# Row sums added to acc by GpSimd instead of VectorE, with every stored row at twice its value until ScalarE halves it in the last pass

## The reference, cut to what matters

```python
def _L0_rec_ref(x, beta, W, b):      # x 2048x512, beta 1024x8x512, W 1024x512, b 1024
    s = einsum('bn,hln->bhl', x, beta)
    ssq = einsum('bn,hln->bhl', x * x, beta * beta)
    fm = 0.5 * sum(s * s - ssq, axis=-1)
    return fm + x @ W.T + b
```

## Time and profile before

| | |
|---|---|
| median of 3 runs | 789.49 us (788.95 to 790.73) |
| the profiled execution, its own time | 789.54 us |
| its span in the trace | 787.8 us |
| busy: PE / PEld / DVE / ACT / POOL | 98% / 80% / 71% / 52% / 47% |
| DMA moved | 145.35 MB, 185 GB/s in the mean |

### The profile page before, as it was taken

The page is one execution under the profiler, slowest core; times in us unless marked ns, Lnnn a source line. Parts: engine busy times, 40 slices in busy tenths (PEclk is TensorE's granted clock), DMA queues, the critical chain, the costliest instruction groups (busy, mean ns, idle before and its releaser), DMA issues. The chain is left out here.

```text
span 787.8 us, 9817 instructions
## 1 busy us (share of the span) xinstructions
PE 774.3 (98%) x3382; PEld 633.7 (80%) x3382; DVE 559.4 (71%) x646; ACT 410.2 (52%) x564; POOL 369.1 (47%) x328
## 2 busy tenths in 40 slices
PE   8999999899999999999999999999999999989998
PEld 5887878688888888888888888888888888867886
DVE  6899468976666666666666765766576656699995
ACT  5665355455554555455555555555555545553330
POOL 0133175446554654465346545653556355434443
PEclk9999999999999999999999999999999999999999
DMA  9596963085624561466046515651663166438933
GB/s 342 212 383 251 363 213 104 15 326 161 228 87 146 199 223 34 147 214 214 27 154 220 208 32 172 229 177 31 218 229 125 47 220 214 148 95 312 382 128 152
DMA packets 66738, 145.35 MB, mean 185 GB/s; under 512 B 4864, under 2 KB 41728, under 8 KB 64384
## 3 DMA queue, kind: packets, MB, share of 16 engines
q1 hardware_dynamic: 66688, 144.72, 52.0%
HBM read 102.76 MB, written 41.94 MB: 184 GB/s over the span
## 5 line engine op out<-in xcount | busy, mean ns | idle before, releaser
L443 PE MATMUL bank<-t_hi,s_hi 128*128 128x512 f32 x1116 | 436.6, 391 | 8.1 <-ACT r L593 3.7
L447 PE MATMUL bank<-t_lo,s_hi 128*128 128x512 f32 x1124 | 438.1, 390 | 0.4 <-DVE t_lo L691 0.2
L449 PE MATMUL bank<-t_hi,s_lo 128*128 128x512 f32 x1116 | 434.7, 390 | 0.0
L443 PEld LDWEIGHTS bank<-t_hi,s_hi 128*128 128x128 f32 x1116 | 209.8, 188 | 57.8 <-ACT r L593 4.5
L447 PEld LDWEIGHTS bank<-t_lo,s_hi 128*128 128x128 f32 x1124 | 211.4, 188 | 44.3 <-DVE t_lo L691 1.0
L449 PEld LDWEIGHTS bank<-t_hi,s_lo 128*128 128x128 f32 x1116 | 209.8, 188 | 43.8
L954 POOL TENSOR_TENSOR r<-r 128x512 f32<-128x512 f32 x70 | 109.7, 1567 | 261.9 <-ACT r L605 261.9
L817 DVE TENSOR_REDUCE sums<-cs 128x128 f32<-128x1024 f32 x128 | 155.4, 1215 | 69.6 <-ACT cs L624 68.7
L801 DVE TENSOR_TENSOR cs<-bank,r 128x512 f32<-128x512 f32 x70 | 48.4, 691 | 85.4 <-PE bank L449 84.9
L958 POOL TENSOR_TENSOR cs<-r 128x512 f32<-128x512 f32 x70 | 92.7, 1324 | 22.0 <-issue 17.0
L950 POOL TENSOR_TENSOR acc<-acc,bias_all 128x128 f32<-128x128 f32 x128 | 60.8, 496 | 87.2 <-DMA acc<-acc_kept 87.1
(11 more groups left out here) (53 smaller groups left out, 343.6 us busy)
## 6 DMA issues: line engine op xcount, KB each, us to landing
s_hi<-s_hi_kept SPq DMA_DIRECT2D x30, 896.0 KB, 5.2
s_lo<-s_lo_kept SPq DMA_DIRECT2D x30, 896.0 KB, 6.9
t_lo_in<-beta_p SPq DMA_DIRECT2D x16, 1024.0 KB, 7.1
s_lo_in<-x_p SPq DMA_DIRECT2D x16, 512.0 KB, 4.3
acc_kept<-cs SPq DMA_DIRECT2D x16, 512.0 KB, 5.4
acc<-acc_kept SPq DMA_DIRECT2D x64, 128.0 KB, 4.8
acc_kept<-acc SPq DMA_DIRECT2D x64, 128.0 KB, 1.8
s_hi_kept<-s_hi SPq DMA_DIRECT2D x8, 896.0 KB, 6.1
```

The costliest lines, as they stand in the source:

```text
L443: nc.tensor.matmul(to, s_hi[:, slot, s_op, cols], hi[:, k, :], start=start, stop=False, skip_group_check=True)
L447: nc.tensor.matmul(to, s_hi[:, slot, s_op, cols], lo[:, k, :], start=False, stop=False, skip_group_check=True)
L449: return nc.tensor.matmul(to, s_lo[:, slot, s_op, cols], hi[:, k, :], start=False, stop=stop, skip_group_check=True)
```

## The change

- All rows that are kept in DRAM hold twice their value. In the W pass ScalarE multiplies by 2 instead of copying, and VectorE's three additions of a bank become one `scalar_tensor_tensor` each (bank times 2 plus the other operand). ScalarE doubles the bias once.
- In the main passes line 823 of VectorE is gone. GpSimd adds `sums` to `acc` in one instruction over 128x256, in group g+1, behind the bias for g+1 and ahead of r5 + r7 of g+1. For group 71 it stands in group 72, behind line 969.
- In the Q pass ScalarE halves each `f` in place, one instruction over 128x2048. The first stands behind `square_row2(71)`, the others at the end of a group for the next one. GpSimd's and VectorE's first use of an `f` waits for that.
- SyncE issues the first six loads of `f` ahead of `store_acc(71)`, where it was two.

```diff
@@ SyncE, Q pass
                 if i == 0:
-                    load_f(0)
-                    load_f(1)
+                    for other in range(6):
+                        load_f(other)
                     store_acc(FIRST_Q - 1)
-                    for other in range(2, 6):
-                        load_f(other)
@@ ScalarE
-                nc.scalar.copy(cs[:, g, row, half, :], bank(g, place)).then_inc(direct_copied, 1)
+                nc.scalar.mul(cs[:, g, row, half, :], bank(g, place), 2.0).then_inc(direct_copied, 1)
+
+            def copy_of(g, to, place):        # used by copy_r1, copy_r5, copy_r7; C11 in the same way
+
+                if g < FIRST_MAIN:
+                    return nc.scalar.mul(to[:, :], bank(g, place), 2.0)
+                return nc.scalar.copy(to[:, :], bank(g, place))
+
+            def halve_f(i):
+                act.wait_ge(f_loaded[i], 16)
+                nc.scalar.mul(f_at(i), f_at(i), 0.5).then_inc(f_halved, 1)
...
                 if g >= FIRST_MAIN:
                     square_12(g)
+                elif g == FIRST_MAIN - 1:
+                    act.wait_ge(bias_loaded, 16)
+                    nc.scalar.mul(bias_all[:, :], bias_all[:, :], 2.0).then_inc(bias_doubled, 1)
             for g in range(FIRST_Q, GROUPS):
                 copy_r1(g)
                 if g == FIRST_Q:
                     square_row2(g - 1)
+                    halve_f(0)
                 for other in groups_for(SUMMED_IN, g):
                     square_x(other)
                     split_s(other)
+                if g + 1 < GROUPS:
+                    halve_f(g + 1 - FIRST_Q)
@@ VectorE
+            def add_from(g, to, place, other):     # used by add_r2, add_c12, add_c21
+
+                if g < FIRST_MAIN:
+                    return nc.vector.scalar_tensor_tensor(to, bank(g, place), 2.0, other[:, :], ALU.mult, ALU.add)
+                return nc.vector.tensor_tensor(to, bank(g, place), other[:, :], ALU.add)
...
@@ VectorE, sum_rows
-                dve.wait_ge(row2_summed, m + 1)
-                dve.wait_ge(acc_biased, m + 1)
-                nc.vector.scalar_tensor_tensor(acc[:, g % 2, :, :], sums[:, :, :], 0.5, acc[:, g % 2, :, :],
-                                               ALU.mult, ALU.add).then_inc(acc_added, 1)
@@ VectorE, Q pass, line 901
-                dve.wait_ge(f_loaded[i], 16)
+                dve.wait_ge(f_halved, i + 1)
@@ GpSimd
+            def add_sums(g):
+
+                m = g - FIRST_MAIN
+                pool.wait_ge(acc_biased, m + 1)
+                pool.wait_ge(row1_summed, m + 1)
+                pool.wait_ge(row2_summed, m + 1)
+                nc.gpsimd.tensor_tensor(acc[:, g % 2, :, :], acc[:, g % 2, :, :], sums[:, :, :], ALU.add
+                                        ).then_inc(acc_added, 1)
...
                     made.then_inc(acc_biased, 1)
+                    if m:
+                        add_sums(g - 1)
                 pool.wait_ge(r5_copied, count(g))
...
-                pool.wait_ge(f_loaded[i], 16)
+                pool.wait_ge(f_halved, i + 1)
...
                 nc.gpsimd.tensor_tensor(f[:, 1, COLS:], f[:, 1, COLS:], r5[:, :], ALU.add).then_inc(o22_added, 1)
+                if i == 0:
+                    add_sums(g - 1)
```

More of the change, by code:

```diff
@@ L213, in fm_layer @@
         row2_summed = sem("row2_summed")
+        bias_doubled = sem("bias_doubled")
+        f_halved = sem("f_halved")
         acc_biased = sem("acc_biased")
@@ L592, in copy_r1 @@
                     act.wait_ge(r2_added, count(g - 1))
-                nc.scalar.copy(r1[:, :], bank(g, BANK_A)).then_inc(r1_copied, 1)
+                copy_of(g, r1, BANK_A).then_inc(r1_copied, 1)
             def copy_r5(g):
@@ L598, in copy_r5 @@
                     act.wait_ge(c22_added, count(g - 1))
-                nc.scalar.copy(r5[:, :], bank(g, BANK_E)).then_inc(r5_copied, 1)
+                copy_of(g, r5, BANK_E).then_inc(r5_copied, 1)
             def copy_r7(g):
@@ L604, in copy_r7 @@
                     act.wait_ge(r57_added, count(g - 1))
-                nc.scalar.copy(r7[:, :], bank(g, BANK_D)).then_inc(r7_copied, 1)
+                copy_of(g, r7, BANK_D).then_inc(r7_copied, 1)
             def take_c11(g):
@@ L610, in take_c11 @@
                 if g < FIRST_MAIN:
-                    nc.scalar.copy(cs[:, g % 2, 0, 0, :], bank(g, BANK_A)).then_inc(c11_taken, 1)
+                    nc.scalar.mul(cs[:, g % 2, 0, 0, :], bank(g, BANK_A), 2.0).then_inc(c11_taken, 1)
                 else:
@@ L794, in add_r2 @@
                     dve.wait_ge(c22_added, count(g - 1))
-                nc.vector.tensor_tensor(r2[:, :], bank(g, BANK_B), r1[:, :], ALU.add).then_inc(r2_added, 1)
+                add_from(g, r2[:, :], BANK_B, r1).then_inc(r2_added, 1)
             def add_c12(g):
@@ L800, in add_c12 @@
                 wait_cs_free(dve, g, 0)
-                nc.vector.tensor_tensor(cs[:, g % 2, 0, 1, :], bank(g, BANK_E), r2[:, :], ALU.add
-                                        ).then_inc(c12_added, 1)
+                add_from(g, cs[:, g % 2, 0, 1, :], BANK_E, r2).then_inc(c12_added, 1)
             def add_c21(g):
@@ L806, in add_c21 @@
                 wait_cs_free(dve, g, 1)
-                nc.vector.tensor_tensor(cs[:, g % 2, 1, 0, :], bank(g, BANK_D), r2[:, :], ALU.add
-                                        ).then_inc(c21_added, 1)
+                add_from(g, cs[:, g % 2, 1, 0, :], BANK_D, r2).then_inc(c21_added, 1)
             def sum_rows(g):
@@ L945, in _ @@
                     if m == 0:
-                        pool.wait_ge(bias_loaded, 16)
+                        pool.wait_ge(bias_doubled, 1)
                     pool.wait_ge(acc_loaded[g % 2], 16 * (m // 2 + 1))
```

## The result

The changed kernel took 806.42 us (median of 4 runs, 804.49 to 807.04) against 789.30 for the kernel before; the ratio is 1.0204, with a 95% interval of 1.0185 to 1.0222. That is 17.1 us more; the forecast was 803, 13.35 more, in a range of 793 to 809. The profiled execution took 804.49 us with a span of 802.7, 14.9 longer than before. The other executions of this kernel were up to 2.6 us longer.

The account below looks back on a forecast made before the run. TensorE was taken to bound the kernel. W pass 0.1, groups 9 to 13 5.0, groups 66 to 72 4.0 and Q pass 4.25 summed to 13.35 us on 789.54, so 803 us; range 793 to 809.

Parts of the forecast that it names:

- What bounds: Whole kernel: TensorE, busy 98% of the span; time saved or spent elsewhere counts only where TensorE waits.
- the three places of the earlier trace: TensorE's losses near groups that prepare an x: 2.31 us at 144.31, 1.35 at 700.31, 1.19 at 723.43.
- the wait at 144.31: TensorE's 2.31 us behind ScalarE's copy of r1, said to cost more as the clock then fell to 0.57.
- The loop: Main passes: addition waits for bias and acc load; nothing in six passes, 5.0 us in groups 9 to 13.
- Price of the addition: GpSimd's new addition over 128x256, taken as 0.75 us, between 0.50 and 1.32.
- Groups 66 to 72: Late stores of acc delay the x for 72 and 73: 4.0 us, bounds 1.5 and 6.
- The meeting with line 691: Groups 66 to 72: GpSimd's addition meets VectorE's line 691 right behind the row sums, 1.2 us.
- The halving: Q pass: ScalarE halves f, 1.91 us each; cycle near 9.98 us, five more groups lose 0.41 each, 2.05.
- The mis-sized term: Start of the Q pass: first f halved before use, making `add_r2(73)` late by 2.2 us, within 1.4 to 2.7.
- Only the Q pass: Rival: load and bias don't bind and x comes in time; 794, or 796 with half another term; chance 0.18.
- Contention everywhere: Rival: collisions with line 691 reach steady passes, or new waits drop the clock; 8 to 10 us more, 812; chance 0.09.
- Faster: Rival: VectorE's relief shrinks the 144.31 wait by 1.9 us, clock holds, Q pass cost hidden; 785.5; chance 0.06.

Follow-up runs that it names:

- e12: Kernel before, all work where it was, but SyncE's store of acc for g-1 also waits for the bias for g: 794.74 us, ratio 1.0058.
- e3: Changed kernel, but GpSimd adds the sums for g-1 ahead of the bias for g, not behind it: 797.65 us, ratio 1.0100.
- e1: Changed kernel, but VectorE keeps the addition of the sums; doubling, halving and new order of f loads stay: 795.40 us, ratio 1.0065.
- e2: Kernel before with the addition on GpSimd behind the bias, one half put into ScalarE's squares, no doubling or halving: 800.80 us, ratio 1.0137.
- e7: e2 with GpSimd's addition ahead of the bias: 793.49 us, ratio 1.0045.
- e11: e7, but VectorE adds for groups 69 to 71 and GpSimd for the other 61: 791.68 us, ratio 1.0024.
- e5: Changed kernel, but ScalarE halves the next group's f ahead of its split of x, not behind it: 804.33 us, ratio 1.0171.

## Why the prediction was right, step by step

- **What bounds.** Right: TensorE, near the three places of the earlier trace rows and nowhere else. 456.96 us of steady passes are equal to the hundredth. Not right is that the wait at 144.31 "costs more than its length" by the fall of the clock; see the last section.
- **The loop.** Right, with its cause shown: e12 has the wait and no work (4.9 us), e3 the work and no wait (1.0 us lost in the main passes). The steps of groups 9 to 12 came as worked out: store of 9 at 118.03 (117.15, or 1 us later), of 10 at 127.55 (127.1), x at 128.01 (127.55), `copy_r1(12)` at 134.53 (134.85), TensorE's wait 3.39 us (3.4 to 4.4). The second fall of the clock that the prediction kept for its upper bound of 8 did come, at 135.14, but TensorE had to wait for r1 again at 149.23 in any case, so 5.2 us were lost and not more.
- **Price of the addition.** 0.74 us alone (0.75 taken), 0.92 in the mean, with its waits for VectorE.
- **Groups 66 to 72.** 3.8 us against 4.0. The meeting with line 691 was there: the addition for group 69 took 1.56 us (698.21), and r5 + r7 behind it 3.07 instead of 1.3.
- **The halving.** Price right (1.91 to 1.92). In e1, where it is alone, `add_r2(73)` came 2.2 us late against P3 of 71 (20.82 us instead of 18.58), and the cycle was 9.99 against 9.98. That this is exactly the 2.2 taken is in part luck: the 2.2 was the middle between a case with and one without an addition of GpSimd among VectorE's sums, and in e1 that addition isn't there, while line 823's still is on VectorE.
- **The mis-sized term** is the one from f to `add_r2(73)`: 4.2 us measured, 2.2 taken, bounds 1.4 to 2.7. The step that failed is "The first f landed at 712.66 ... in the same order as before. Now ScalarE halves it first: 714.6": I moved f with TensorE's lag and left its landing as it was. It landed 1.6 us later than that. The other 0.4 is the chain behind it, 2.6 us longer, near the upper of the two cases, with GpSimd's addition (728.52) among VectorE's sums of x. So GpSimd's half of the change costs time in the Q pass too: e2 and e7 show it with no halving at all (1.5 and 2.5 us), and e11, where VectorE adds for the last three groups, has nothing of it left (0.1 us). That it works through the late store for 70 and the x behind it fits the traces, but was not tested by itself.
- **From the trace to the median.** The profiled execution lost 14.9 us, the median 17.1. The profiled one was the fastest of the four, with the highest mean clock (0.991, against 0.989 in the one that took 807.04 and 0.985 in the one of 806.99). How often the clock fell may be part of the difference, but the two don't go in step, and only one run has a trace. The forecast had added the places up for a profiled execution and taken the median as 0.05 us away from it; this distance of 1.9 us is in no term of it.
- **Rivals.** Only the Q pass: ruled out by the 5.2 and 3.8 us that were lost ahead of it; e1, in which nothing else costs, took 795.4 against its 794. Contention everywhere: ruled out by the steady passes. The Trainium skill ("GPSIMD Engine Reference", Key points) says that GpSimd and VectorE contend where VectorE has two SBUF inputs, and the trace agrees: the addition takes up to 1.56 us there instead of 0.74, nine times in the steady passes too, but in those TensorE never waited for it. Faster: VectorE's relief never reached TensorE, not even in e7 (793.49), where neither the loop nor the halving stood in its way.

## What to carry to other kernels

An operation moved to another engine takes over that engine's queue: look at what stands in front of it there (here the bias, waiting for a load), and whether the thing waited for depends in turn on the operation's own last result. Such a loop cost nothing in the steady passes, where its round was longer than a group (by the prediction's estimate) in only half of the groups and x was loaded three groups ahead; but where it started late, and an x was still to be prepared, it delayed every transfer queued behind it. A long in-place pass over data belongs in a gap of its engine, not between two steps of a chain: the same halving cost 0.4 us a group behind the split and none ahead of it. Nor does moving a piece of work out of a chain give back its whole length: in e5 VectorE's own split took the place of the 1.9 us of halving, and 0.4 us came back.

## What the runs showed of the hardware that I had not expected

The granted clock after an idle stretch of TensorE did not follow its length. Before, the 4 us behind 2.31 us of idling had 0.57, that is mostly the level of 1.2 GHz. In e1 TensorE idled 2.32 us at the same place (its matmul at 143.92), in e7 even 2.87 us (143.66), and in neither did the clock fall: it was 1.00 from 140 to 152 us in both. The windows around the wait in e7 (columns as in the earlier trace rows):

```profile
140.00:144.00 4.00, 1.13 (x5) 0.62 (x4) 3.81 (x6) 1.50 (x3) 0.79 (x1) 1.00 0.00 0
144.00:148.00 4.00, 2.63 (x12) 1.83 (x11) 3.84 (x4) 4.00 (x6) 2.01 (x3) 1.00 0.09 26
```

In after, 3.39 us (135.14), 2.43 (149.23) and 4.74 (734.57) each came with a fall; in the third the clock was low before the idling ended (0.56 from 732 to 736):

```profile
136.00:140.00 4.00, 3.91 (x12) 2.64 (x12) 3.92 (x3) 4.00 (x7) 2.53 (x2) 0.68 0.01 3
148.00:152.00 4.00, 2.77 (x6) 1.83 (x6) 3.69 (x5) 3.93 (x5) 0.45 (x1) 0.60 0.00 0
...
736.00:740.00 4.00, 4.00 (x12) 3.19 (x11) 3.23 (x6) 0.00 (x0) 3.20 (x3) 0.59 1.00 372
```

What the fall in the kernel before cost can be read from e1, which has none there. Its groups 8 to 15 took 81.49 us (86.29 to 167.78, by the `q_part` instructions), the kernel before 81.66 (86.62 to 168.28). At the full clock TensorE only came earlier to its next wait, the 1.36 us at 146.94. So a fall that slows matmuls in front of another wait costs next to nothing, here 0.2 us at most. The times of the kernel before agree: in one series six runs with a mean clock of 1.000 took 787.57 to 789.81 us, five with 0.997 took 788.69 to 790.10, but five with 0.996 took 790.39 to 791.97. Where the clock fell in those last five no trace shows.

Runs of one kernel differ too: e1's six took 793.12 to 796.82 us with mean clocks of 0.991 to 0.998, though not in step (796.03 us at 0.998, 794.78 at 0.991). So one trace is not enough to price a stall of 2 to 3 us.
